# Adaptive-norm block with causal attention and routed experts on one core: setup loads by first use, norms three steps later, slot rows ahead of weights

## The chip, the cores and the metric

The kernel runs on one NeuronCore of a Trainium2 chip: TensorE (PE) for matrix products, VectorE (DVE), ScalarE (ACT) and GpSimd (POOL) for the rest, SyncE (SP) as the queue that issues most transfers, and 16 DMA engines that move data between HBM and the on-chip memory. Each engine runs its own instructions in order, and semaphores tie them together. The metric is the device time of one launch in microseconds (us). Three runs of the kernel before took 746.2, 750.95 and 752.59 us: the median is 750.95.

## The reference, cut to what matters

Eight sequences of 512 tokens of width 128. A conditioning vector per sequence, through SiLU and one matrix, gives six rows: shift, scale and gate for attention and for the feed-forward part. Cut to its core:

```
mod = (silu(c) @ wmod).reshape(8, 6, 1, 128)       # sa, ca, ga, sb, cb, gb; the gates kept >= 0.25 in size
h = layernorm(x) * (1 + ca) + sa
# attention block on h: layer norm; Q, K, V = x U V + b per head, 16 heads of 8, rank 48; causal softmax;
#   out_U out_V + out_b; second layer norm; low-rank MLP with gelu
x = x + ga * attention_block(h)
h = layernorm(x) * (1 + cb) + sb
# feed-forward: RMS norm; a shared MLP with relu; sigmoid router, the best 2 of 8 experts for each token
x = x + gb * (shared(h) + routed(h))
```

All of it is kept in 32-bit floats, but for the attention scores, where Q and K are split into three bf16 parts each.

## The kernel before

**Setup.** SP issues the loads of c, of the matrix w_mod (128 x 768), of the first three sequences of x (512 B per token row) and of the small weights; ACT's queue issues the low-rank factors u_t of Q, K and V (96 rows of 12,288 B, in two halves) and v_t. ACT, DVE and PE form SiLU(c) and its product with w_mod (L1120 the first 256 columns, L1121 the other 512), L1126 spreads the rows of two sequences over the partitions, and L1133 multiplies the low-rank factors of all three of Q, K and V pair by pair (`ps_s2`, 48 products) into `w_qkv`, which DVE copies out (L1554). DVE, with POOL for the reciprocal roots (L738, L740: `var_eps`, `rstd`), norms sequences 0 and 1 before the steps begin. `gates()` (L1520 to L1531) makes the gates from the other columns. `small_weights` (L1155 to L1158) multiplies out_U out_V and the two low-rank factors of the MLP, and DVE copies the results out (L1566 to L1570).

**Attention.** One step n for each group of four heads of one sequence, 32 groups in all, from step -9 on: a table of offsets (`T_AT`, `Q_AT`, ..., `STATS_AT`, `NORM_AT`) says in which step, counted from 4b, each piece of work for sequence b is done. In a step PE makes the first scores of group n+3 (L1205, L1208) that DVE reduces to row maxima (L1620, 12 per step); POOL splits the maxima into bf16 parts (L799 to L807), PE transposes them (L1214), ACT empties them (L987), and SP stores them in HBM and loads them into the Q stack (L575, L585). The second scores of group n (L1232, L1236) then carry their maximum, ACT takes exponentials (L958), and PE makes the context (L1253). Between these, PE transposes, projects and splits the next sequence: Q and K go through ACT, POOL (L787, L791; DVE for sequence 0) and SP (L545 to L551 store them, `load_stack` at L565 and L567 loads them as stacks). The norms of sequences 2 to 7 are four pieces of DVE work in four successive steps (`layer_norm`, after the 4th and the 8th row maximum): statistics of x; scale and shift; statistics of h; normalise. ACT also writes zeros and ones into the Q stacks and the V tiles (L942, L945) before the first step. POOL's step ends with the roots, then adds the two biases to h (L840, L847) where they are due, behind the context's normalisation (L825).

**Experts.** After the MLP and the shared part, tokens are scattered by POOL into regions of HBM by expert (L880), SP pads each region by 132 KB of filling rows (L694, L696, 8 of them), and 39 tiles of 256 slots run: SP loads the tile's rows (`load_slots`, L703, L704) and its expert's weights (`load_weights`, L711 to L713, 514 KB and 64 KB) into four buffers, PE turns the rows (L1390), multiplies (L1428, L1438), ACT and DVE finish, and POOL scatters the results (L926). Before tile 0's second product PE also finishes the shared part of sequences 6 and 7 (L1346): the turn of tile 0 stands ahead of the last 16 of these products in PE's queue.

## Time and profile before

| what | value |
|---|---|
| median of 3 runs | 750.95 us (746.2 to 752.59) |
| the profiled execution's own time | 749.43 us |
| its span, first to last instruction | 747.6 us |
| mean granted TensorE clock | 0.94 of full |
| busy: PE, DVE, ACT, POOL | 624.8, 443.2, 421.0, 304.7 us |
| first exponential of the attention | 75.8 us after the start |
| first product of the expert tiles (L1428) | 570.7 us |

The profile gives, for one execution, the busy time of every engine, the chain of waits that ended last, groups of instructions with their durations and what released the engine before them, and the transfers with the time from issue to landing. A busy PE is not PE at its peak, so shares over the whole span say little; what bounds a stage is read in that stage. Setup lasts until the first exponential, attention until about 395 us, the MLP, shared part and routing until about 560 us, and the expert tiles until about 710 us.

### The profile page before, as it was taken

To read this page: it belongs to the slowest core of one execution; us is meant where nothing else is said; L and a number is where in the kernel's file an instruction comes from. 1 tells how busy PE (TensorE), PEld (TensorE's weight loads), DVE (VectorE), ACT (ScalarE), POOL (GpSimd) and SP (SyncE) were. 2 spreads that over 40 slices of the span, in tenths; PEclk is the share of its full clock that TensorE was granted. 3 is DMA by queue.
4 is the path that set the end of the run, shared out by engine and by line. 5 is a ranking of instruction groups with operands and counts; after the bars stand their busy time and mean duration, and the time that the engine had idled before them with its cause. 6 is when DMAs were issued, how large, how long until landed. Compare 5 with 4: busy or idle time off the path is not lost.

```text
span 747.6 us, 15319 instructions
## 1 busy us (share of the span) xinstructions
PE 624.8 (84%) x5334; PEld 413.5 (55%) x5365; DVE 443.2 (59%) x1306; ACT 421.0 (56%) x749; POOL 304.7 (41%) x490
## 2 busy tenths in 40 slices
PE   4756899998998989999979777887976999999940
PEld 3523444444444544444436464666746899999930
DVE  2689687878788766777606676666741222222227
ACT  5321667676666657666675767775423555555510
POOL 4141424143433415131314276755740454455541
PEclk9958999999999999999999988998997999999975
DMA  8542232333243423331834112111163777777827
GB/s 176 190 162 75 80 123 98 133 133 108 100 158 108 150 91 132 133 106 50 247 118 126 54 46 73 52 47 44 59 164 95 228 229 230 229 226 228 229 104 267
DMA packets 85853, 100.97 MB, mean 135 GB/s; under 512 B 12960, under 2 KB 68040, under 8 KB 85680
## 3 DMA queue, kind: packets, MB, share of 16 engines
q1 hardware_dynamic: 76752, 87.19, 37.9%
q0 software_dynamic: 4544, 9.45, 3.5%
q10 hardware_dynamic: 4480, 3.35, 1.9%
q8 instruction: 43, 0.70, 0.4%
q14 instruction: 34, 0.28, 0.1%
HBM read 60.28 MB, written 37.57 MB: 131 GB/s over the span
## 4 chain that ended last, share of the span: by engine, by line
PE 52%; DVE 12%; DMA 10%; SPq 8%; issue 6%; POOL 5%; ACT 5%; another core or an unknown queue 0%; POOLq 0%; ACTq 0%; DVEq 0%
PE ps_r L1438 8%; PE ps_s L1428 8%; PE ps_pv L1253 7%; DVE row_max L1620 4%; PE ps_r L1208 4%; PE ps_pv L1324 3%; PE ps_r L1205 3%; PE ps_s L1316 3%; DMA arena<-slots_d 3%; PE ps_s L1236 2%; PE ps_r L1346 2%; PE ps_s L1332 2%; DMA k_d<-arena_early 2%; PE ps_pv L1346 2%; PE ps_r L1183 2%
## 5 line engine op out<-in xcount | busy, mean ns | idle before, releaser
L1620 DVE TENSOR_REDUCE row_max<-ps_r 128x1 f32<-128x384 f32 (+3 forms) x384 | 207.0, 595 | 67.6 <-PE ps_r L1208 59.5
L958 ACT ACTIVATE arena<-ps_s 128x1024 f32<-128x1024 f32 (+1 forms) x192 | 159.1, 880 | 64.0 <-PE ps_s L1236 63.1
L1205 PE MATMUL ps_r<-later_q,ident_b 128*128 128x128 bf16 (+1 forms) x384 | 92.5, 247 | 29.8 <-DVE row_max L1620 18.2
L926 POOL DMA_INDIRECT y_d<-arena,target x78 | 74.7, 957 | 94.8 <-DVE arena L1813 82.6
L1208 PE MATMUL ps_r<-arena 128*128 128x128 bf16 (+3 forms) x481 | 112.1, 302 | 0.0
L1205 PEld LDWEIGHTS ps_r<-later_q,ident_b 128*128 128x128 bf16 x384 | 36.1, 98 | 90.2 <-DVE row_max L1620 43.5
L1253 PE MATMUL ps_pv<-arena 128*32 128x512 f32 (+3 forms) x1024 | 83.3, 444 | 0.1
L1809 DVE TENSOR_TENSOR arena<-ps_r,arena_early 128x256 f32<-128x256 f32 x39 | 16.6, 425 | 107.6 <-PE ps_r L1438 107.6
L880 POOL DMA_INDIRECT slots_d<-arena,slots x64 | 65.0, 1015 | 27.5 <-issue 17.7
L1236 PE MATMUL ps_s<-arena 51*128 51x256 bf16 (+3 forms) x512 | 60.2, 300 | 0.0
L1208 PEld LDWEIGHTS ps_r<-arena 128*128 128x128 bf16 x512 | 51.3, 100 | 13.9 <-issue 3.2
L1438 PEld LDWEIGHTS ps_r<-arena 128*128 128x128 f32 x480 | 58.2, 192 | 1.5
L1438 PE MATMUL ps_r<-arena 128*128 128x128 f32 x480 | 58.3, 275 | 0.0
L1110 ACT ACTIVATE arena<-ps_s,arena 128x256 f32<-128x256 f32 x120 | 50.4, 471 | 13.5 <-PE ps_s L1428 12.8
L1428 PE MATMUL ps_s<-arena 128*128 128x256 f32 x240 | 56.8, 379 | 0.0
L799 POOL TENSOR_SCALAR neg_part<-row_max 128x16 bf16<-128x16 f32 x32 | 8.2, 256 | 99.4 <-DVE row_max L1620 99.4
L1428 PEld LDWEIGHTS ps_s<-arena 128*128 128x128 f32 x240 | 43.3, 190 | 4.6
L1253 PEld LDWEIGHTS ps_pv<-arena 128*32 128x32 f32 x1024 | 26.9, 110 | 32.2 <-issue 25.8
L1232 PE MATMUL ps_s<-ident_h,lower_k 64*128 64x64 bf16 (+1 forms) x384 | 40.0, 205 | 5.4 <-ACT arena L958 4.9
L738 POOL TENSOR_TENSOR var_eps<-moments,ln_eps 128x4 f32<-128x4 f32 x24 | 4.9, 202 | 86.3 <-DVE moments L1449 86.3
L1232 PE MATMUL ps_s<-ident_h,upper_k 64*128 64x64 bf16 (+1 forms) x384 | 38.9, 199 | 0.0
L1324 PE MATMUL ps_pv<-w_fc,arena 128*128 128x128 f32 x256 | 33.9, 296 | 5.5 <-ACT arena L1048 5.5
(221 smaller groups left out, 1113.1 us busy)
## 6 DMA issues: line engine op xcount, KB each, us to landing
arena<-in_ew SPq DMA_DIRECT2D x30, 514.0 KB
ctx_d<-ctx_raw SPq DMA_DIRECT2D x32, 256.0 KB, 3.4
arena<-q_d SPq DMA_DIRECT2D x64, 102.0 KB
arena<-k_d SPq DMA_DIRECT2D x64, 96.0 KB
arena<-slots_d SPq DMA_DIRECT2D x39, 132.0 KB, 3.2
arena_early<-in_ew SPq DMA_DIRECT2D x9, 514.0 KB
arena<-y_d SPq DMA_DIRECT2D x8, 512.0 KB, 6.2
q_d<-arena_early SPq DMA_DIRECT2D x8, 384.0 KB, 3.0
```

What stands on the lines that cost most here:

```text
L880: pool.indirect_dma_start(slots_d[:], bass.IndirectOffsetOnAxis(ap=slots[:, c, i:i + 1], axis=0), n3x[:, c, i, :], None).then_inc(scattere ...
L926: pool.indirect_dma_start(y_d[:], bass.IndirectOffsetOnAxis(ap=target[:, k, c:c + 1], axis=0), res[:, k, c, :], None).then_inc(put[k], 16)
L958: act.activation(dst, src, ACT.Exp, scale=SCALE).then_inc(exp_done, 1)
L1205: pe.matmul(diag, ident_b[:], later_q[:].unsqueeze(1).to_broadcast([P, len(js), P]), start=True, stop=False, skip_group_check=True)
L1208: mm = pe.matmul(bnk[:, k * keys:(k + 1) * keys], q_st[b % 2][:, g, j, i * P:(i + 1) * P], k_st[b % 2][:, g, j // 2, 0:keys], start=False, ...
L1232: pe.matmul(banks[half][:, :, at:at + HALF], stationary[whole], near, start=(at == 0), stop=False, skip_group_check=True)
L1236: mm = pe.matmul(banks[j % 2][:, k // 2, :], k_st[b % 2][rows, g, j // 2, kt * P:(kt + 1) * P], q_st[b % 2][rows, g, j, kt * P:S], start=F ...
L1253: mm = pe.matmul(ps_pv[32 * j:32 * j + 32, kt * P:S], v_sb[b % 2][:, kt, GROUPS * j + g, :], probs[:, p % 2, at:at + length], start=(kt == ...
L1324: mm = pe.matmul(ps_pv[:, i * P:(i + 1) * P], hidden[:, k, i * P:(i + 1) * P], w_fc2[:, k, :], start=(k == 0), stop=(k == NF - 1))
L1428: mm = pe.matmul(ps_s2[:, 2 * (k % 2) + f // 2, (f % 2) * SLOTS:(f % 2 + 1) * SLOTS], x_w[k][:, f * P:(f + 1) * P], tok_t[:, k], start=Tru ...
L1438: mm = pe.matmul(ps_s1[:, k % 2, c * P:(c + 1) * P], x_hidden[:, k, f, c * P:(c + 1) * P], x_w[k][:, FF + f * D:FF + (f + 1) * D], start=( ...
L1620: dve.reduce_max(row_max[:, m % 2, js[0] % 2, j:j + len(js), i], src, AXIS.X).then_inc(max_taken, 1)
```

## The change

**Setup loads.** SP's first loads become c, x of sequence 0, the first 256 columns of w_mod, the small columns, x of sequence 1, the other 512 columns of w_mod. u_t is loaded without V's third at first (rows of 8,192 B), V's third follows on ACT's queue behind the exponential of c. The product with w_mod waits only for its 256 columns. The products with the other 512 columns and those of V's pairs move on PE into `small_weights`, behind the first projections of Q and K; ACT in place of DVE empties three of the small weights and writes the V tiles' ones there. `gates()` moves behind DVE's step -3, and the store of its rows from step -3 to -2. Sequence 2 is normed in setup as well, and the four pieces of norm work for sequences 3 to 7 each stand three steps later.

**First stack.** The stores of sequence 0's Q have a semaphore of their own, so that the loads of group 0's Q rows go out before K's stores have landed.

**Experts.** SP issues four fillings, the weights of tile 0, four more fillings, then waits for the fillings and the scatters, then the rows of tiles 0 and 1 and the weights of 1, rows of 2, weights of 2, and so on; before, all four weights went ahead of the wait and of all rows.

```diff
 T_AT, Q_AT, K_AT, K_OUT_AT, LOAD_AT, V_AT = -9, -9, -8, -7, -6, -3
 CTX_AT, REC_AT, OUT_AT = 6, 7, 8
 AFTER_STATS_AT, AFTER_NORM_AT, AFTER_T_AT, AFTER_OUT_AT = 9, 10, 10, 11
-NORM_EARLY = 2
-SMALL_STEP, BIAS_STEP, MOD_STEP = -7, -4, -3
-STATS_AT, SCALE_AT, H_STATS_AT, NORM_AT = -16, -15, -14, -13
+NORM_EARLY = 3
+SMALL_STEP, BIAS_STEP, MOD_STEP = -7, -4, -2
+STATS_AT, SCALE_AT, H_STATS_AT, NORM_AT = -13, -12, -11, -10
...
-                    sp.dma_start(w_mod, a["w_mod"]).then_inc(c_loaded, 16)
-                    for b in range(2):
-                        sp.dma_start(x_sb[:, NT * b:NT * (b + 1), :], x_tok[:, NT * b:NT * (b + 1), :]).then_inc(x_loaded[b], 16)
+                    sp.dma_start(x_sb[:, 0:NT, :], x_tok[:, 0:NT, :]).then_inc(x_loaded[0], 16)
+                    sp.dma_start(w_mod[:, 0:2 * D], a["w_mod"][:, 0:2 * D]).then_inc(w_mod_loaded, 16)
+                    sp.dma_start(cols[:], a["cols"]).then_inc(cols_loaded, 16)
+                    sp.dma_start(x_sb[:, NT:2 * NT, :], x_tok[:, NT:2 * NT, :]).then_inc(x_loaded[1], 16)
+                    sp.dma_start(w_mod[:, 2 * D:6 * D], a["w_mod"][:, 2 * D:6 * D]).then_inc(small_loaded, 16)
...
+                            stored_q = q_stored if b == 0 else qk_stored
+                            sp.dma_start(dst[:, 0:3], part[:, 0:3]).then_inc(stored_q, 16)
+                            sp.dma_start(dst[:, 3:5], part[:, 0:2]).then_inc(stored_q, 16)
+                            sp.dma_start(dst[:, 5:6], part[:, 0:1]).then_inc(stored_q, 16)
...
-                    def load_stack(b, g):
-
-                        wait(sp, qk_stored, 16 * 6 * (b + 1))
+                    def load_stack(b, g, of="qk"):
+
+                        if b == 0:
+                            sp.wait_ge(q_stored, 48)
+                        if "k" in of:
+                            sp.wait_ge(qk_stored, 16 * (6 * b + 3))
...
-                                load_stack(b, g)
+                                load_stack(b, g, "k" if b == 0 and g == 0 else "qk")
...
+                            if batch_at(n, K_OUT_AT) == 0:
+                                load_stack(0, 0, "q")
...
-                    sp.wait_ge(fill_known, 1)
-                    for e in range(E):
-                        at = sp.value_load(fill_at[0:1, e:e + 1], min_val=N_REGION * SLOTS * e, max_val=N_REGION * SLOTS * e + B * S)
-                        chunk = (SPARE_ROWS + SLOTS * e) // P
-                        sp.dma_start(slots_d[bass.ds(at, SLOTS), :].rearrange("(c p) w -> p c w", p=P), fill[:, chunk:chunk + SLOTS // P, :])\
-                            .then_inc(slots_filled, 16)
-
                     def load_slots(t):
 
...
+                    sp.wait_ge(fill_known, 1)
+                    for e in range(E // 2):
+                        store_fill(e)
                     sp.wait_ge(mapped, 2)
-                    for t in range(BUF):
+                    load_weights(0)
+                    for e in range(E // 2, E):
+                        store_fill(e)
+                    sp.wait_ge(scattered, 2 * 16 * B * NT)
+                    sp.wait_ge(slots_filled, 16 * (E + 1))
+                    load_slots(0)
+                    for t in range(1, BUF):
+                        load_slots(t)
                         load_weights(t)
-                    sp.wait_ge(slots_filled, 16 * (E + 1))
-                    sp.wait_ge(scattered, 2 * 16 * B * NT)
-                    for t in range(BUF):
-                        load_slots(t)
...
-                    for b in range(2):
+                    for b in range(NORM_EARLY):
                         x_rstd_of(b)
...
-                        act.dma_start(u_t[HALF * half:HALF * half + RANK], a["u_t"][rows]).then_inc(pairs_loaded, 16)
+                        act.dma_start(u_t[HALF * half:HALF * half + RANK, 0:2], a["u_t"][rows, 0:2]).then_inc(pairs_loaded, 16)
                         act.dma_start(v_t[HALF * half:HALF * half + RANK], a["v_pairs"][half]).then_inc(pairs_loaded, 16)
-                    act.wait_ge(c_loaded, 32)
+                    act.wait_ge(c_loaded, 16)
                     act.activation(c_exp, c_t, ACT.Exp, scale=-1.0).then_inc(c_exped, 1)
+                    for half in range(2):
+                        rows = slice(RANK * half, RANK * half + RANK)
+                        act.dma_start(u_t[HALF * half:HALF * half + RANK, 2], a["u_t"][rows, 2]).then_inc(small_loaded, 16)
                     act.wait_ge(v_zeroed, 1)
                     for stack in q_st:
                         act.activation(stack[:].rearrange("p g j s -> p (g j s)").bitcast(F32), zeros[:, 0:1].to_broadcast([P, GROUPS * JH * S // 2]), ACT.Copy)\
                             .then_inc(q_zeroed, 1)
-                    for v in v_sb:
-                        act.activation(v[:].rearrange("p i h e -> p (i h e)"),
-                                       zeros[:, 0:1].to_broadcast([P, NT * HEADS * 32]), ACT.Copy, bias=1.0).then_inc(v_ones, 1)
+                    def ones_of_v():
+                        for v in v_sb:
+                            act.activation(v[:].rearrange("p i h e -> p (i h e)"),
+                                           zeros[:, 0:1].to_broadcast([P, NT * HEADS * 32]), ACT.Copy, bias=1.0).then_inc(v_ones, 1)
 
...
+                        if n == SMALL_STEP:
+                            ones_of_v()
+                            act.wait_ge(small_done, 1)
+                            act.activation(w_out[:], ps_s2[:, 0, 0:D], ACT.Copy).then_inc(small_copied, 1)
+                            act.activation(w_fc1[:], ps_s2[:, 2, :], ACT.Copy).then_inc(small_copied, 1)
+                            act.activation(w_fc2[:].rearrange("p k d -> p (k d)"), ps_s2[:, 3, :], ACT.Copy).then_inc(small_copied, 1)
...
+                    pe.wait_ge(w_mod_loaded, 16)
                     pe.matmul(ps_m[0:B, 0:2 * D], c_silu, w_mod[:, 0:2 * D], start=True, stop=True).then_inc(mod_done, 1)
-                    pe.matmul(ps_pv[0:B, 0:512], c_silu, w_mod[:, 2 * D:6 * D], start=True, stop=True).then_inc(mod_done, 1)
                     pe.wait_ge(consts2, 1)
                     pe.wait_ge(mod_copied, 1)
                     pe.wait_ge(mod_ready, 1)
                     for b in range(2):
                         pe.matmul(wide_rows(b), ident[0:B, b:b + 1].to_broadcast([B, P]), mod[:, 0:2, :], start=True, stop=True).then_inc(mod_wide, 1)
+
+                    def pairs(*ms):
+                        for m in ms:
+                            for k in range(PAIRS):
+                                for half in range(2):
+                                    rows = slice(HALF * half, HALF * half + RANK)
+                                    at = DH * (PAIRS * m + k)
+                                    mm = pe.matmul(ps_s2[:, half, at:at + DH], u_t[rows, m, k, :], v_t[rows, m, k, :], start=True, stop=True)
+                        mm.then_inc(pairs_done, 1)
+
                     pe.wait_ge(pairs_loaded, 64)
-                    for m in range(3):
-                        for k in range(PAIRS):
-                            for half in range(2):
-                                rows = slice(HALF * half, HALF * half + RANK)
-                                at = DH * (PAIRS * m + k)
-                                mm = pe.matmul(ps_s2[:, half, at:at + DH], u_t[rows, m, k, :], v_t[rows, m, k, :], start=True, stop=True)
-                    mm.then_inc(pairs_done, 1)
+                    pairs(0, 1)
...
                         pe.wait_ge(small_loaded, 16 * SMALL)
+                        pairs(2)
+                        pe.matmul(ps_pv[0:B, 0:512], c_silu, w_mod[:, 2 * D:6 * D], start=True, stop=True).then_inc(mod_done, 1)
                         pe.wait_ge(w_qkv_ready, 6)
...
-                    dve.wait_ge(pairs_done, 1)
-                    for m in range(3):
+
+                    def keep_pairs(m):
                         order = "p (e k t) -> p t k e" if m < 2 else "p (k t e) -> p t k e"
                         kept = w_qkv[:, m, :].rearrange(order, k=PAIRS, t=2)
                         for half in range(2):
                             at = PAIRS * DH * m
                             dve.tensor_copy(kept[:, half], ps_s2[:, half, at:at + PAIRS * DH].rearrange("p (k e) -> p k e", e=DH))\
                                 .then_inc(w_qkv_ready, 1)
+
+                    dve.wait_ge(pairs_done, 1)
+                    keep_pairs(0)
+                    keep_pairs(1)
                     norm_all(1)
+                    stats_all_x(2)
 
                     for m in range(2):
                         dve.wait_ge(act_emptied, BY_ACT["QK"[m], 0] + 1)
...
                         dve.wait_ge(qk_mid, m + 1)
                         dve.tensor_tensor(qk_part[:, m, 2], qk_rest[:, m], qk_part[:, m, 1], ALU.subtract).then_inc(qk_low, 1)
                     normalise_all(1)
-                    gates()
-                    dve.wait_ge(small_done, 1)
-                    dve.tensor_copy(w_out[:], ps_s2[:, 0, 0:D]).then_inc(small_copied, 1)
+                    dve.wait_ge(pairs_done, 2)
+                    keep_pairs(2)
+                    norm_all(2)
                     dve.wait_ge(cols_loaded, 16)
                     dve.tensor_scalar(vb_wide, zeros[:], col("v_b"), None, ALU.add).then_inc(small_copied, 1)
-                    dve.tensor_copy(w_fc1[:], ps_s2[:, 2, :]).then_inc(small_copied, 1)
-                    dve.tensor_copy(w_fc2[:].rearrange("p k d -> p (k d)"), ps_s2[:, 3, :]).then_inc(small_copied, 1)
+                    dve.wait_ge(mod_done, 2)
+                    dve.tensor_copy(mod[:, 2:6, :], ps_pv[0:B, 0:512].rearrange("b (k d) -> b k d", d=D)).then_inc(mod_copied, 1)
+                    normalise_all(2)
 
...
+                        if n == MOD_STEP - 1:
+                            gates()
```

Three places where the order of instructions moves. First, TensorE at the program's start (`ps_m` is `ps_r`, `ps_pv` takes the 512 columns; `in_*` and `arena` hold the loaded weights). Before:

```order
L1120 MATMUL ps_r<-arena 8x256 [waits silu_ready]
L1121 MATMUL ps_pv<-arena 8x512
L1126 MATMUL ps_s<-arena,ident 128x256 [waits mod_ready,mod_copied,consts2]
L1126 MATMUL ps_s<-arena,ident 128x256
L1133 MATMUL ps_s<-arena 128x8 [waits pairs_loaded]
L1133 MATMUL ps_s<-arena 128x8 x47
L1169 MATMUL ps_r<-ident,arena_early 128x128 [waits xn_ready,consts2]
```

And now:

```order
L1147 MATMUL ps_r<-arena 8x256 [waits w_mod_loaded,silu_ready]
L1152 MATMUL ps_s<-arena,ident 128x256 [waits mod_ready,mod_copied,consts2]
L1152 MATMUL ps_s<-arena,ident 128x256
L1160 MATMUL ps_s<-arena 128x8 [waits pairs_loaded]
L1160 MATMUL ps_s<-arena 128x8 x31
L1201 MATMUL ps_r<-ident,arena_early 128x128 [waits xn_ready,consts2]
```

The 512-column product and 16 of the 48 pair products have left the stretch ahead of the first transposes; they stand behind the projections of Q and K.

Second, GpSimd ahead of the first split of row maxima: the Q and K remainders of sequence 1 (`arena_early` tiles) and the roots of the norms. Before:

```order
L738 TENSOR_TENSOR var_eps<-moments,ln_eps 128x4 [waits h_moments]
L740 TENSOR_TENSOR rstd<-var_eps,half_neg 128x4 [waits h_eps]
L787 TENSOR_TENSOR arena_early<-arena_early 128x512 [waits qk_low,act_emptied]
L791 TENSOR_TENSOR arena_early<-arena_early 128x512 [waits qk_mid]
L787 TENSOR_TENSOR arena_early<-arena_early 128x512 [waits qk_low,act_emptied]
L738 TENSOR_TENSOR var_eps<-moments,ln_eps 128x4 [waits x_moments]
L740 TENSOR_TENSOR rstd<-var_eps,half_neg 128x4 [waits x_eps]
L791 TENSOR_TENSOR arena_early<-arena_early 128x512 [waits qk_mid]
L799 TENSOR_SCALAR neg_part<-row_max 128x16 [waits max_taken]
```

And now:

```order
L752 TENSOR_TENSOR var_eps<-moments,ln_eps 128x4 [waits h_moments]
L754 TENSOR_TENSOR rstd<-var_eps,half_neg 128x4 [waits h_eps]
L796 MEMSET rms_eps 128x4
L797 MEMSET per_d 128x4
L801 TENSOR_TENSOR arena_early<-arena_early 128x512 [waits qk_low,act_emptied]
L805 TENSOR_TENSOR arena_early<-arena_early 128x512 [waits qk_mid]
L801 TENSOR_TENSOR arena_early<-arena_early 128x512 [waits qk_low,act_emptied]
L805 TENSOR_TENSOR arena_early<-arena_early 128x512 [waits qk_mid]
L813 TENSOR_SCALAR neg_part<-row_max 128x16 [waits max_taken]
```

The root of sequence 3 no longer stands between the remainders of sequence 1; that of sequence 2 still stands ahead of them.

Third, SyncE's queue ahead of the expert tiles (`in_ew` the expert's weights, `slots_d` the sorted rows). Before:

```order
L711 TENSOR_LOAD tile_expert [waits mapped]
...
L712 DMA arena<-in_ew 128x1028
...
L713 DMA arena_early<-in_eb 128x128
...
L712 DMA arena_early<-in_ew 128x1028
...
L703 TENSOR_LOAD tile_row [waits scattered,slots_filled]
...
L704 DMA arena<-slots_d 128x264
```

And now:

```order
L713 TENSOR_LOAD tile_expert [waits mapped]
...
L714 DMA arena<-in_ew 128x1028
...
L721 DMA slots_d<-arena 128x2x132
...
L705 TENSOR_LOAD tile_row [waits slots_filled,scattered]
...
L706 DMA arena<-slots_d 128x264
L705 TENSOR_LOAD tile_row
...
L706 DMA arena<-slots_d 128x264
L713 TENSOR_LOAD tile_expert
```

Three of the four weight loads ahead of tile 0's rows are now behind them, and four of the fillings are behind the first weights.

## Rows read from the trace of the kernel before

**Rows 1.** Transfers issued in the first 60 us: issues, KB each, median us to landing
```profile
arena<-in_u_t ACTq DMA_DIRECT2D x2, 576.0 KB, 8.7
x_sb<-in_x SPq DMA_DIRECT2D x3, 256.0 KB, 12.1
arena<-in_w_mod SPq DMA_DIRECT2D x1, 384.0 KB, 7.5
arena<-in_c_t SPq DMA_DIRECT2D x1, 4.0 KB, 4.4
```

**Rows 2.** Chain of waits, 0 to 80 us: start, us, what
```profile
1.23 7.54 DMA arena<-in_w_mod
...
9.70 1.02 PE ps_r L1120 x2
10.72 1.71 PE ps_pv L1121 x2
12.43 2.00 PE ps_s L1126 x4
14.43 10.34 PE ps_s L1133 x96
...
46.86 1.12 POOL arena_early L787
...
51.27 1.01 POOL rstd L740
...
65.63 4.51 DMA max_d<-max_rows
```

**Rows 3.** Instructions in order of time: start, us, engine, line, [idle before, releaser]
```profile
15.92 3.69 ACT L945 ACTIVATE arena<-zeros 128x2048 f32<-128x2048 f32 x2
...
31.89 1.05 PE L1158 MATMUL ps_s<-arena 64*128 64x128 f32 x8
...
34.69 1.11 DVE L1483 TENSOR_SCALAR arena_early<-h_sb,moments,rstd 128x128 f32<-128x128 f32 x4
...
37.84 2.07 PE L1183 MATMUL ps_r<-arena_early,w_qkv 128*128 128x512 f32 x2 [0.87 <-ACT arena_early L965]
...
38.53 0.67 DVE L1569 COPY w_fc<-ps_s 128x512 f32<-128x512 f32 x1
```

**Rows 4.** The same view in the attention steps: DVE in step 0
```profile
83.40 1.02 DVE L1620 TENSOR_REDUCE row_max<-ps_r 128x1 f32<-128x384 f32 x2 [3.33 <-PE ps_r L1208]
```

**Rows 5.** Chain of waits, 78 to 260 us: the shift of a norm in step 1
```profile
94.81 1.05 DVE h_sb L1472 x4
```

**Rows 6.** GpSimd in order of time, 165 to 245 us: steps 11 and 15
```profile
198.02 1.26 POOL L840 TENSOR_TENSOR h_sb<-h_sb,fc_bias 128x512 f32<-128x512 f32 x1
...
200.49 0.25 POOL L799 TENSOR_SCALAR neg_part<-row_max 128x16 bf16<-128x16 f32 x1
...
242.47 0.25 POOL L799 TENSOR_SCALAR neg_part<-row_max 128x16 bf16<-128x16 f32 x1 [1.34 <-DVE row_max L1620]
```

**Rows 7.** Instructions in order of time ahead of the expert tiles, 540 to 606 us
```profile
544.22 8.58 SPq L696 DMA_DIRECT2D slots_d<-arena  x8
...
553.57 0.38 SPq L712 DMA_DIRECT2D arena<-in_ew  x1
...
560.55 4.74 SPq L704 DMA_DIRECT2D arena<-slots_d  x5
565.50 0.69 PE L1390 MATMUL ps_r<-ident,arena 128*128 128x128 f32 x2 [8.58 <-DMA arena<-slots_d]
```

**Rows 8.** The fillings' line L696, 540 to 566 us
```profile
DMA to landing us min/median/max: 2.1/2.3/2.8
```

**Rows 9.** The page's transfers: all 39 loads of slot rows, KB each, median us to landing
```profile
arena<-slots_d SPq DMA_DIRECT2D x39, 132.0 KB, 3.2
```

**Rows 10.** Windows: busy us of PE, PEld, DVE, ACT, POOL; granted clock, DMA share, GB/s
```profile
560.10:570.20 10.10, 4.10 (x18) 3.81 (x18) 0.56 (x1) 0.47 (x1) 0.00 (x0) 0.50 0.56 180
...
650.00:700.00 50.00, 49.93 (x346) 46.76 (x345) 12.81 (x52) 28.92 (x68) 25.69 (x27) 1.00 0.78 228
```

35 lines of the change are left out of this document (19 added, 16 removed).

## The prediction

> **What bounds the kernel now.** I read the chain of waits first, then the instructions in order of time around its long pieces, then the transfers and the windows. Three stretches matter.
>
> Setup, 0 to 80 us. The chain begins with the landing of w_mod, which is issued at 1.23 us and takes 7.54 us [rows 2]; SiLU follows, then four stretches of PE without a gap: the 256-column product (1.02), the 512-column product (1.71), the spread of rows (2.00) and the pair products (10.34 for 96 passes, 0.108 us each), which end at 24.77 us [rows 2]. From there it runs through ACT and PE to POOL, whose remainder of sequence 1 starts at 46.86 us [rows 2], and through SP's stores and loads to the first maximum's store at 65.63 us [rows 2]. That store blocks ACT, and with it PE's transposes of sequence 2; the first exponential comes at 75.8 us. So setup is a latency chain: an edit counts only where it shortens this chain.
>
> Attention steps, about 10.3 us each. PE and DVE are both in the chain; DVE's norm work shows there in pieces [rows 5], but in steps that project K it waits for PE, once 3.33 us [rows 4].
>
> Experts. In 650 to 700 us PE is busy 49.93 of 50 us at a DMA share of 0.78 [rows 10]: the tiles are bound by PE, and what can be won is their start. PE idles 8.58 us for the first tile's rows and turns them at 565.50 [rows 7].
>
> **The change part by part.**
>
> *Loads and pair products.* The 256-column product starts at 9.70 us now. Afterwards the exponential needs only c, which lands 4.4 us after its issue [rows 1], so SiLU is done by about 6.1, and the 256 columns of w_mod (128 KB) decide. Ahead of them stand 256 KB of x in rows of 512 B, so as many bytes as now (384 KB) must pass on SP's queue before they have landed. By bytes they land at 8.8 us like w_mod now (1.23 + 7.54), and the product starts 0.9 us early. But x took 12.1 us to land and finished only with u_t [rows 1]: small rows pass slowly beside u_t's long ones. If the x rows wait for u_t again, which is two thirds as long, the columns land at about 11. I take a start at 9.7 as now, between 8.8 and 11.
>
> Then the 512-column product is gone from the path. Now the spread of rows starts 12.43 − 9.70 = 2.73 us after the first product; without it, it must wait for that product (1.02) and DVE's two copies (about 0.5 us), so 1.55: **1.2 us** gained. Of 96 pair passes 32 move: 32 x 0.108 = **3.45 us**. The spread then ends at 13.2 and the pairs at 20.2. DVE's norm of sequence 0 was hidden behind the pairs and nearly is still: x has landed, statistics start at 11.2, and by the same durations as now the normalised rows are ready at 19.7. Cover left: 0.5 us. Sum 4.6 us; I take **4.5**, bounds 3.2 and 5.8 (by the landing).
>
> *From the projections to the first maximum's store*, in today's times. The moved pair products (3.45 us) and the 512 columns (1.7) run on PE from about 30.3 to 35.5, beside the split of Q and K; DVE normalises sequence 1 till 35.8 [rows 3], copies V's pairs (0.3), and PE's small weights (2.6 us long, ending now at 32.94 [rows 3]) end at 38.7. ACT's ones (3.69 us [rows 3]) lie in 34.05 to 37.7 before that, covered by 1.0 us. ACT empties the small weights in 0.27 + 2 x 0.67 = 1.6 us (DVE's duration [rows 3], for ACT's I have none) till 40.3, then sequence 1's transposes (0.79), PE projects Q (2.07 at the lower clock [rows 3]) till 43.2, ACT's two copies take 1.3: POOL can start at 44.5. Now it starts at 46.86 [rows 2], since it waits for the root of sequence 2, whose norm DVE begins only at 39.72; after the change that root is done at 40.8. Gain 2.4 us. Then the root of sequence 3 (1.24 us with its addition [rows 2]) no longer stands between the remainders. Gain 1.2. SP is free in time, since group 0's Q rows go out during K's stores. Sum **3.6 us**, bounds 1.5 and 5 (PE at either clock, and SP's 16 stack loads). The first steps' DVE work is 5.7 us lighter (one sequence's norm), and `gates()` adds 1.8 between two of them; the maximum's own path ends by 60 us, before SP is ready for it at 62. So the first exponential comes 4.5 + 3.6 = **8.1 us** early.
>
> *Norms three steps later.* Nothing is added; each piece meets other work. The shift (1.05 us in the chain [rows 5]) leaves the steps that project V for the ones that project K, where DVE waits for PE anyway [rows 4]; statistics take its place. In GpSimd's queue the root of x now stands behind the context's normalisation, which waits for a transfer, and ahead of L840 and L847: in step 11 they end at 200.49 and delays the next maximum already [rows 6], so 1.25 us are lost there, while in step 15 it has 1.34 us to spare [rows 6]. Sequence 7's norm falls on steps 15 to 18, which had less. I set gains of 0.7 us in four steps against 1.25 + about 1.5 and take **0**, bounds +4 lost and 3 gained.
>
> *Experts.* Fillings come every 1.17 us from 544.22 (8 in 8.58 [rows 7]), weights every 1.7 (four between 553.57 and 560.55 [rows 7]). Four fillings, one weight (issued at 548.8), four fillings: the last issue is at 553.9, landed 2.8 us later at the most [rows 8], 556.7; the last of POOL's scatters ends its issue at 552.9, so it isn't later. The tile number's load takes 0.7, so tile 0's rows go out at 557.4, not 560.55. They took 4.9 us then, queued behind three to four weights of 514 KB; the median of all 39 such loads is 3.2 [rows 9]. With one weight ahead, long landed, I take 3.2: the turn comes at 560.7 and not 565.5: **4.8 us**, bounds 3.1 (if the load still takes 4.9) and 5.5. The weights of tiles 1 to 3 go out at about 559, 562 and 564.5; PE wants them at 567.7, 571.4 and 575 (3.73 us per tile). The clock doesn't help: it was at the lower level, 0.50 of full, from 560.10 to 570.20 [rows 10], after PE had idled from 556.9, and PE will idle 3.7 us still.
>
> Sum: 8.1 + 0 + 4.8 = 12.9 us. The profiled execution took 749.43 us, so 736.5; the median of the runs is 1.5 us above it, which would give 738. I predict **737 us**.
>
> A rule of the Trainium skill speaks about the first term (DMA: Bandwidth & Descriptors, Queues, rings and completion order): a DMA engine takes turns between queues packet by packet, a packet being some 9 to 17 descriptors, so that x's small rows would not be held up row for row by u_t's long ones. The landing of x with u_t [rows 1] speaks against it; by the rule the sum would be 2.7 us better, as the fourth case below.
>
> **The rivals.**
>
> 1. *The front is eaten downstream* (12%). The stack loads or K's stores land later because everything now goes out closer together, and the first maximum's store stays near 63 us. For it: the chain passes four transfers here. Then about 2 us of the 8.1 remain: 749.4 − 2 − 4.8 = 742.5.
> 2. *The tiles start early and starve* (10%). Weights of tiles 1 to 3 share the engines with rows and put PE to wait: 710 KB per tile at 228 GB/s [rows 10] are 3.1 us, so 3.7 us of slack must be used up. All of the 4.8 us would go: 741.5.
> 3. *Slower* (5%). GpSimd's queue in every fourth step: the root of x can start only after DVE's 8th maximum, and L840, L847 and the next split wait behind it. Full price 1.25 + 1.26 + 1.27 = 3.8 us (L847 takes as long as L840 [rows 6]) in steps 3, 7, 11 and 15, 15.2 us, and the shift in the K steps shows in full, 5 x 1.05. 749.4 − 12.9 + 20.4 = 757. It decides from the point where the split ends more than about 4 us after DVE's last maximum, where PE transposes; against it stands the slack of step 15 [rows 6].
> 4. *Columns early* (10%). The 256 columns land at 7, beside u_t. The spread starts at 8.6, pair products wait for u_t till 10.6, and end at 17.5 instead of 20.2: 734.
> 5. *It doesn't do what it says* (3%): all the waits are replaced by others, 749.
>
> The forecast has 60%, with its own range of 731 to 743: the bounds of the four terms seldom meet at one end.
>
> **How the numbers follow.** About 1% (7.5 us) is what a measurement of this kernel can tell from no change, so faster means under 743.4. The forecast and case 4 give nearly all of their 70%, cases 1 and 2 about 13 of 22 points: 82% faster. The rest of these and case 5 make 13% same. Slower 5%. The range reaches from 731 to 745: it takes in case 4 and cases 1 and 2 for the most part, and leaves out case 3, case 5 and the far ends.
>
> **What would show it.** The 256-column product near 9.7 us (case 4: near 7), and the first transposes of sequence 0 near 20.2. POOL's first remainder of sequence 1 near 40, the first maximum's store near 57.5, the first exponential near 67.7. Distances of the maxima's splits in attention as before within 0.5 us, with steps 11 and 15 the ones to look at. The turn of tile 0 4.8 us closer to the first filling's store than now (21.3 us), and no wait of PE for weights in tiles 1 to 3. I would be wrong if PE's pair products wait for u_t or x, if ACT's ones hold up the transposes of sequence 1, or if the gain at the first exponential isn't there any more when the attention ends.

## The result: 0.994 of the time before, where 0.98 was forecast

| | before | after |
|---|---|---|
| median of the runs | 751.26 us (20 runs) | 747.61 us (20 runs) |
| ratio, 95% interval | | 0.9942 (0.9920 to 0.9963) |
| profiled execution, span | 749.43, 747.6 us | 749.93, 748.1 us |

In a second comparison, where all kernels ran on one chip (`all_before`, `all_after` below), the ratio was 0.9931 (0.9903 to 0.9959). So the change gains 4 to 5 us. Forecast were 737 us and a range up to 745; the time lies outside it.

### Profile after: setup

The chain of waits of the changed kernel, 0 to 80 us (start, us, what); these answer to [rows 2]:

```profile
1.70 8.07 DMA arena<-in_w_mod
...
9.91 1.03 PE ps_r L1147 x2
...
11.59 2.04 PE ps_s L1152 x4
13.62 6.93 PE ps_s L1160 x64
20.55 1.06 PE ps_r L1201 x4
...
34.70 1.72 PE ps_s L1190 x8
...
41.87 1.16 POOL arena_early L801
...
59.65 4.25 DMA max_d<-max_rows
```

The 256 columns land at 9.77 us, their product starts at 9.91 (9.70 before), and the first transposes come at 20.55, where the pairs before ended at 24.77: 4.2 us earlier. The remainder of sequence 1 starts 5.0 us earlier (41.87 against 46.86), the first maximum's store 6.0 (59.65 against 65.63). The first exponential comes at 69.6 us, 6.2 earlier than 75.8.

One piece of this chain is longer than before. The two passes of one product of the small weights (L1156 before, L1188 after), in order of time:

```profile
30.88 1.17 PE L1156 MATMUL ps_s<-arena 64*128 64x512 f32 x2
32.63 2.07 PE L1188 MATMUL ps_s<-arena 64*128 64x512 f32 x2
```

All the small weights together (12 passes) took 2.6 us before and take 4.5 now (31.90 to 36.41). They take 4.5 in every trace of a kernel with the new setup, e1_norms_back and the later ones included, and 2.6 to 3.1 in the four traces with the old one. The cause is TensorE's lower clock: the clock rows of the changed kernel's first trace don't begin until 51 us, but in seven of the others they cover this stretch, and read 0.50 of full, as in e1_norms_back (PE, PEld, DVE, ACT, POOL busy, then the granted clock, DMA share, GB/s):

```profile
32.20:36.70 4.50, 4.48 (x13) 2.99 (x13) 3.88 (x18) 1.55 (x1) 1.22 (x4) 0.50 0.57 190
```

### Profile after: attention

What follows uses one number per step: the distance from one split of maxima to the next, taken between the starts of GpSimd's first row of each split (L799 before, L813 after; 32 of them). The length of step n runs from the split that ends step n-1 to the one that ends step n; the first split ends step -3, the last one step 28. The first split is 6.8 us earlier than before; the last is 6.8 us later (377.77 against 370.99). Steps 1 to 28, called "attention" in what follows, take 294.5 us (83.31 to 377.77), before 282.8 (88.23 to 370.99). **Here the gain of setup goes, and as much again.**

GpSimd in order of time at the end of step 11 (start, us, engine, line, operation; in brackets the idle time before it and its releaser); it answers to [rows 6]:

```profile
196.45 1.27 POOL L839 TENSOR_TENSOR ctx_n<-ctx_t,rec_rows 128x512 f32<-128x512 f32 x1 [5.51 <-DMA rec_rows<-rec_d]
197.67 0.20 POOL L752 TENSOR_TENSOR var_eps<-moments,ln_eps 128x4 f32<-128x4 f32 x1
197.95 1.04 POOL L754 TENSOR_TENSOR rstd<-var_eps,half_neg 128x4 f32<-128x4 f32 x1
198.96 1.27 POOL L854 TENSOR_TENSOR h_sb<-h_sb,fc_bias 128x512 f32<-128x512 f32 x1
200.20 1.26 POOL L861 TENSOR_TENSOR h_sb<-h_sb,out_bias 128x512 f32<-128x512 f32 x1
201.43 0.26 POOL L813 TENSOR_SCALAR neg_part<-row_max 128x16 bf16<-128x16 f32 x1
```

No gap between them: the root's two instructions stand in the chain between a transfer (`rec_rows`) and the next split. In step 15 the same rows run from 242.94 to 247.97, and the split that had 1.34 us to spare before [rows 6] has none.

DVE and GpSimd in order of time in step 4, which projects K:

```profile
115.14 2.04 DVE L1499 SCALAR_TENSOR_TENSOR arena_early<-x_sb,moments,arena_early 128x128 f32<-128x128 f32 x4
115.76 1.27 POOL L805 TENSOR_TENSOR arena_early<-arena_early 128x512 bf16<-128x512 f32 x1 [0.74 <-ACT arena_early L996]
...
118.72 1.02 DVE L1656 TENSOR_REDUCE row_max<-ps_r 128x1 f32<-128x384 f32 x2 [0.62 <-PE ps_r L1240]
119.66 2.03 DVE L1504 SCALAR_TENSOR_TENSOR h_sb<-arena_early,rstd 128x128 f32<-128x128 f32 x4
119.85 1.17 POOL L801 TENSOR_TENSOR arena_early<-arena_early 128x512 f32<-128x512 f32 x1 [2.82 <-ACT arena_early L992]
121.62 2.47 DVE L1656 TENSOR_REDUCE row_max<-ps_r 128x1 f32<-128x512 f32 x4
...
122.35 0.23 PE L1237 MATMUL ps_r<-later_q,ident_b 128*128 128x128 bf16 x1 [1.53 <-DVE row_max L1656]
```

And the same group of four shifts in the kernel before, in step 5, which projects V:

```profile
134.75 1.13 DVE L1472 SCALAR_TENSOR_TENSOR h_sb<-arena_early,rstd 128x128 f32<-128x128 f32 x4
```

Step 4 of the kernel before, which has no shift, shows where DVE waits for TensorE: 0.92 us ahead of the 7th maximum, and only 0.28 behind the 8th:

```profile
124.10 1.02 DVE L1620 TENSOR_REDUCE row_max<-ps_r 128x1 f32<-128x384 f32 x2 [0.92 <-PE ps_r L1208]
125.03 0.37 DVE L1449 BATCH_NORM_AGGREGATE moments<-stats 128x2 f32<-128x6 f32 x4
125.68 2.49 DVE L1620 TENSOR_REDUCE row_max<-ps_r 128x1 f32<-128x512 f32 x4 [0.28 <-PE ps_r L1208]
```

Two things are to be seen. In the changed kernel DVE's wait for TensorE still stands ahead of the 7th and 8th maxima (0.62 us), and the shifts stand behind the 8th: they fill no such wait, they make TensorE wait (1.53 us). And four shifts take 2.03 us, not 1.13, while GpSimd's L801 runs beside them. By the line's own view for 119 to 122 us, one of the four took 1247 ns and the others about 340:

```profile
L1504 DVE SCALAR_TENSOR_TENSOR h_sb<-arena_early,rstd x4: 338/341/1247, 119.7 to 121.4; 128x128 f32<-128x128 f32 x4
```

The scale of this step (L1499) meets GpSimd's L805 in the same way and takes 2.04 us. That costs nothing here: e9_shift_sixth below keeps it (2.03 us), and its step 4 is as short as before.

### Profile after: experts

Instructions in order of time, 548 to 575 us; these answer to [rows 7]:

```profile
550.55 3.85 SPq L721 DMA_DIRECT2D slots_d<-arena  x4
...
556.91 4.13 SPq L721 DMA_DIRECT2D slots_d<-arena  x4
...
564.00 1.50 SPq L706 DMA_DIRECT2D arena<-slots_d  x2
...
566.25 0.53 PE L1422 MATMUL ps_r<-ident,arena 128*128 128x128 f32 x2 [2.97 <-DMA arena<-slots_d]
```

From the first filling's store to the turn of tile 0 it is 15.7 us now, 21.3 before: 5.6 us gained, 4.8 forecast. TensorE waits 2.97 us for the rows and not 8.58. The rows of tile 0 go out 13.5 us after the first filling, where 13.2 were forecast, and are turned 2.3 us later, where 3.2 were set. From tile 0's first product to the end of the span it is 176.9 us in both kernels.

### The profile page after: what moved, and what is told of

The parts are those of the page before. It is cut to its first block, busy times and chain, and to the rows that moved or that the text cites. A ratio compares the mean times of both kernels' runs of the same rounds, so it can differ in the third digit from the quotient of the medians.

```text
span 748.1 us, 15358 instructions
## 1 busy us (share of the span) xinstructions
PE 631.9 (84%) x5365; PEld 416.7 (56%) x5365; DVE 445.9 (60%) x1303; ACT 421.2 (56%) x752; POOL 306.6 (41%) x490
## 4 chain that ended last, share of the span: by engine, by line
PE 42%; DMA 16%; SPq 12%; DVE 10%; POOL 8%; issue 6%; ACT 5%; POOLq 0%; ACTq 0%; DVEq 0%
PE ps_r L1470 7%; PE ps_s L1460 7%; PE ps_pv L1285 4%; DMA max_d<-max_rows 4%; PE ps_pv L1356 3%; DMA arena<-slots_d 3%; DVE row_max L1656 3%; DMA k_d<-arena_early 2%; SPq L571 2%; PE ps_s L1348 2%; PE ps_r L1378 2%; SPq L574 2%; PE ps_r L1215 2%; PE ps_s L1364 2%; PE ps_r L1240 2%
## 5 line engine op out<-in xcount | busy, mean ns | idle before, releaser
L1240 PE MATMUL ps_r<-arena 128*128 128x384 bf16 (+3 forms) x512 | 121.3, 310 | 0.0
L1285 PE MATMUL ps_pv<-arena 128*32 128x512 f32 (+3 forms) x1024 | 85.0, 450 | 0.1
L813 POOL TENSOR_SCALAR neg_part<-row_max 128x16 bf16<-128x16 f32 x32 | 8.3, 260 | 112.7 <-DVE row_max L1656 112.5
L1356 PE MATMUL ps_pv<-w_fc,arena 128*128 128x128 f32 x256 | 35.8, 307 | 3.9 <-ACT arena L1074 3.9
L1356 PEld LDWEIGHTS ps_pv<-w_fc,arena 128*128 128x128 f32 x256 | 34.7, 221 | 6.4 <-ACT arena L1074 6.4
```

Of the source, the lines that this page charges most:

```text
L1240: mm = pe.matmul(bnk[:, k * keys:(k + 1) * keys], q_st[b % 2][:, g, j, i * P:(i + 1) * P], k_st[b % 2][:, g, j // 2, 0:keys], start=False, ...
L1285: mm = pe.matmul(ps_pv[32 * j:32 * j + 32, kt * P:S], v_sb[b % 2][:, kt, GROUPS * j + g, :], probs[:, p % 2, at:at + length], start=(kt == ...
L1356: mm = pe.matmul(ps_pv[:, i * P:(i + 1) * P], hidden[:, k, i * P:(i + 1) * P], w_fc2[:, k, :], start=(k == 0), stop=(k == NF - 1))
```

## The experiments

The length of single steps, and of attention (steps 1 to 28), in us. K marks the steps that project K.

| kernel | 4 (K) | 5 | 7 | 8 (K) | 11 | 12 (K) | 15 | 16 (K) | attention |
|---|---|---|---|---|---|---|---|---|---|
| before | 10.51 | 10.11 | 9.85 | 10.81 | 11.55 | 10.51 | 11.35 | 10.55 | 282.8 |
| after | 11.82 | 10.94 | 11.04 | 11.82 | 12.03 | 11.84 | 13.51 | 11.83 | 294.5 |
| e1_norms_back | 10.52 | 10.10 | 9.74 | 10.82 | 11.74 | 10.52 | 11.45 | 10.53 | 284.1 |
| e2_shift_alone | 11.82 | 9.39 | 11.03 | 11.81 | 12.42 | 11.83 | 13.34 | 11.82 | 292.4 |
| e5_root_first | 11.83 | 9.39 | 9.75 | 12.11 | 11.27 | 11.82 | 12.08 | 11.83 | 287.5 |
| e6_stats_only | 10.53 | 10.11 | 10.67 | 10.53 | 12.64 | 10.53 | 11.59 | 10.53 | 285.4 |
| e7_scale_in_k | 11.81 | 9.39 | 10.48 | 11.90 | 12.08 | 12.37 | 11.25 | 10.51 | 290.2 |
| e8_bias_moved | 10.52 | 10.17 | 10.13 | 10.82 | 10.16 | 10.82 | 11.03 | 10.82 | 283.3 |
| e9_shift_sixth | 10.53 | 9.39 | 10.56 | 10.89 | 11.80 | 10.53 | 12.80 | 10.54 | 284.6 |
| e12_no_collision | 10.92 | 9.39 | 10.86 | 10.93 | 12.05 | 10.95 | 12.78 | 10.93 | 285.8 |
| e10_both | 10.51 | 9.39 | 9.75 | 10.89 | 11.25 | 10.65 | 12.03 | 10.64 | 282.4 |
| all_before | 10.51 | 10.10 | 10.17 | 10.81 | 11.55 | 10.54 | 12.21 | 10.51 | 283.5 |
| all_after | 11.82 | 9.39 | 10.87 | 11.81 | 12.11 | 11.81 | 13.47 | 12.93 | 290.3 |

The two traces of the kernel before show how far a step can be trusted: the K steps and step 5 agree within 0.04 us, steps 7 and 15 only within 0.3 and 0.9.

Ratios are to the kernel before on the same chip (medians there: 753.6 for e1 to e4, 751.2 for e5 to e8, 766.0 for e9 to e12, 751.7 for the last four).

### The parts apart

`e1_norms_back`, the changed kernel with one line undone:

```diff
-STATS_AT, SCALE_AT, H_STATS_AT, NORM_AT = -13, -12, -11, -10
+STATS_AT, SCALE_AT, H_STATS_AT, NORM_AT = -16, -15, -14, -13
```

> The changed kernel with one line undone: the four pieces of norm work at offsets -16, -15, -14, -13 again, sequence 2 still normed in setup. Theory A (the new places lengthen the attention steps: the root of x stands ahead of L854 and L861 in GpSimd's queue in every fourth step, and scale and shift stand in the steps that project K): the 13 us that attention lost between the first split of maxima and step 17 come back, about 735 us (733 to 738), and the splits keep their lead of about 6 us over the kernel before to the end of the attention. Theory B (attention is paced by something that a 6 us earlier start cannot move, so the lead would be eaten wherever the norms stand): about 747, as the changed kernel.

Measured: ratio 0.9828 (0.9798 to 0.9858), 13.0 us less than before; the lead at the last split is 2.8 us. Theory A holds (attention 284.1), B falls. The 735 us were not reached (741.7, where before is 753.6), as the size was taken from one trace and the lead was not kept whole: with sequence 3's norm back in the first steps, the first split comes 2.2 us later than in the changed kernel, so the later norms help ahead of step 0.

`e2_shift_alone` is the kernel before with the opposite edit:

> The kernel before with that one line alone changed: offsets -13, -12, -11, -10, sequence 2's norm included. Theory A: 751.3 + 13 = 764 (760 to 767), the added time in the steps up to 17. Theory B: about 751, since no lead is there to be eaten.

Measured: ratio 1.0107 (1.0074 to 1.0141), 8 us slower; attention 9.6 us longer. A's direction is right, its 13 us too much. The kernel has no lead to lose, so this excludes theory B a second time.

`e3_experts_alone`, the kernel before with SyncE's new order ahead of the tiles:

```diff
+for e in range(E // 2): store_fill(e)
 sp.wait_ge(mapped, 2)
-for t in range(BUF): load_weights(t)
-sp.wait_ge(slots_filled, 16 * (E + 1)); sp.wait_ge(scattered, 2 * 16 * B * NT)
-for t in range(BUF): load_slots(t)
+load_weights(0)
+for e in range(E // 2, E): store_fill(e)
+sp.wait_ge(scattered, 2 * 16 * B * NT); sp.wait_ge(slots_filled, 16 * (E + 1))
+load_slots(0)
+for t in range(1, BUF): load_slots(t); load_weights(t)
```

> The kernel before with the new order of SyncE ahead of the expert tiles alone. From the traces of both kernels, first filling's store to first product of tile 0: 26.5 us before, 20.7 after, so 5.8 us less: about 745.5 (744 to 748). If the tiles starve for weights instead, 750 or above.

Measured: ratio 0.9881 (0.9847 to 0.9915), 9 us less; the trace shows 5.6 (filling to first product 20.9 us, 26.5 before). The interval's near end is 6.4; what the rest is, no trace shows. The tiles don't starve.

`e4_setup_alone` is e1_norms_back with the old order of SyncE ahead of the tiles:

> The new setup and first stack with sequence 2 normed in setup, norm offsets and experts as before. The first maximum's store was 6.0 us earlier in the changed kernel and the first exponential 6.2: theory A says 751.3 - 6.2 = 745 (743 to 747). Theory B: 750 or above, since the lead is eaten in the attention.

Measured: ratio 0.9903 (0.9878 to 0.9927), 7.3 us less, as A says. e3 and e4 add up to 16.3 where both together (e1) gave 13.0: within their intervals, and not settled closer.

### What in the later norms costs

`e5_root_first`, the changed kernel with GpSimd's root of x ahead of the context's normalisation:

```diff
+later = batch_at(n, STATS_AT)
+if later is not None and later >= NORM_EARLY:
+    x_rstd_of(later)
 if batch_at(n, REC_AT) is not None:
     ...
     pool.tensor_tensor(ctx_n[:], ctx_t[:], rec_rows[:], ALU.mult)
 ...
-for offset, of in ((STATS_AT, x_rstd_of), (H_STATS_AT, h_rstd_of)):
+for offset, of in ((H_STATS_AT, h_rstd_of),):
```

> The changed kernel with the root of x (L752, L754) issued on GpSimd ahead of the context's normalisation (L839), for which GpSimd waits 5 to 7 us there anyway. Theory C (the root stands in the chain, 1.24 us before L854, L861 and the next split): steps 7, 11 and 15 (11.04, 12.03, 13.51 us from split to split) shorten by 1.0 to 1.25 each, the kernel by 3 us. Theory D (DVE's statistics of x, moved into the same steps, are what lengthens them): they keep their lengths within 0.3 and the time stays.

GpSimd at the end of step 15 of this kernel:

```profile
237.61 0.20 POOL L752 TENSOR_TENSOR var_eps<-moments,ln_eps 128x4 f32<-128x4 f32 x1 [5.51 <-DVE moments L1484]
237.90 1.04 POOL L754 TENSOR_TENSOR rstd<-var_eps,half_neg 128x4 f32<-128x4 f32 x1
238.95 1.26 POOL L842 TENSOR_TENSOR ctx_n<-ctx_t,rec_rows 128x512 f32<-128x512 f32 x1
240.17 1.27 POOL L857 TENSOR_TENSOR h_sb<-h_sb,fc_bias 128x512 f32<-128x512 f32 x1
241.40 1.28 POOL L864 TENSOR_TENSOR h_sb<-h_sb,out_bias 128x512 f32<-128x512 f32 x1
242.64 0.26 POOL L813 TENSOR_SCALAR neg_part<-row_max 128x16 bf16<-128x16 f32 x1
```

The root now lies in what was waiting. Steps 7, 11 and 15 are 1.3, 0.8 and 1.4 us shorter than in the changed kernel: theory C, though by more than the 1.0 to 1.25 expected in two steps and by less in one. The whole time hardly moved (0.9929, 0.9900 to 0.9958): in this profile step -1 took 12.4 us in place of 8.8, with TensorE's granted clock at 0.50 of full (1.2 of 2.4 GHz) from 65 to 70 us, so this run alone doesn't show the gain at the end.

`e6_stats_only` and `e7_scale_in_k` move one piece at a time, starting from e1_norms_back:

```diff
-STATS_AT, SCALE_AT, H_STATS_AT, NORM_AT = -16, -15, -14, -13
+STATS_AT, SCALE_AT, H_STATS_AT, NORM_AT = -17, -15, -14, -13   # e6_stats_only
+STATS_AT, SCALE_AT, H_STATS_AT, NORM_AT = -17, -16, -14, -13   # e7_scale_in_k
```

> As e1_norms_back, but the statistics and the root of x one step earlier (-17 in place of -16), so that this piece alone stands in the steps 3, 7, 11 and 15, as in the changed kernel. If this piece makes their added length: steps 7, 11 and 15 as in the changed kernel (11.0, 12.0, 13.5 us; 9.7, 11.7, 11.5 in e1_norms_back), 3 to 4 us more in all. If normalise's leaving them pays for it in the changed kernel and not here, 1 us more than that. Steps 0, 4, 8, 12 and 16 as in e1_norms_back or shorter by up to 0.3.

> As e6_stats_only, but scale and shift one step earlier too (-16), so that they stand in the steps that project K (4, 8, 12, 16), as in the changed kernel. If DVE's shift between two maxima makes the 1.3 us there: steps 4, 8, 12 and 16 1.3 us longer than in e6_stats_only (10.5 to 11.8 where measured from step 4), the steps behind them 0.75 shorter: 2 to 3 us more in all. My prediction had DVE waiting for PE there, so nothing added and 1.05 us less in the steps behind: 3 us less.

Measured: e6 0.9881 (0.9851 to 0.9911), e7 0.9884 (0.9857 to 0.9912). e6: steps 7 and 11 are 0.9 us longer than in e1_norms_back. Step 15 is only 0.1 longer, but it says nothing of the root: in this kernel no statistics and no root of x stand there (GpSimd runs only L839, L854 and L861), against what was expected of the edit. Attention is 1.3 us longer, where 3 to 4 were expected. e7: steps 4, 8 and 12 are 1.3, 1.4 and 1.8 us longer than in e6; step 16, which holds no shift in this kernel, is unchanged; step 5 is 0.7 shorter; attention 4.7 us more, a part of which is the lower clock, which fell in steps 8 and 12 (3.4 us at 0.50 each). So scale and shift in a K step cost 1.3 us: the opposite of the prediction. The two ratios don't tell them apart; the steps do.

`e9_shift_sixth` and `e12_no_collision` ask why. e9 issues the shifts after the 6th maximum. e12 leaves them behind the 8th, but GpSimd's L801 waits for them:

```diff
-if u in (3, 7):
+if u in (3, 5, 7):        # e9: scale at u == 3, shift at u == 5, all other pieces as before
     layer_norm(n, u)
```

```diff
 if b is not None:
+    shifted = batch_at(n, SCALE_AT)          # e12
+    if shifted is not None and shifted >= NORM_EARLY:
+        pool.wait_ge(h_ready, NT * (shifted + 1))
     qk_remainder(b, 1)
```

> The changed kernel with the four shifts (L1504) after the 6th row maximum of their step in place of the 8th. In step 4 of the changed kernel DVE waits 0.62 us for TensorE between the 6th and 8th maxima, and the shifts behind the 8th take 2.03 us (1.13 in the kernel before), with GpSimd's L801 (1.17 us) running beside them from 119.85. Theory F (the shift costs because it stands behind the wait and collides with L801): after the 6th maximum it takes 1.13 us and fills the wait, so steps 0, 4, 8, 12 and 16 go from 11.8 to about 10.5 us, and the kernel is 5 to 6.5 us faster than the changed one. If all DVE work in such a step costs its own time wherever it stands: 11.8 stays, or at most 0.3 less.

> The changed kernel, shifts after the 8th maximum as there, but GpSimd's second remainder (L801) of these steps waits for them. It tells the collision from the place. If the two engines exclude each other, the shifts take 1.13 us in place of 2.03, and steps 4, 8, 12 and 16 go from 11.8 to 10.9; about 4 us less than the changed kernel in all. If it is the place alone: 11.8 or above, since L801 starts 1 us later and nothing is won.

DVE in step 4 of e9_shift_sixth, with GpSimd's L801:

```profile
116.74 1.01 DVE L1658 TENSOR_REDUCE row_max<-ps_r 128x1 f32<-128x384 f32 x2
...
117.67 1.13 DVE L1504 SCALAR_TENSOR_TENSOR h_sb<-arena_early,rstd 128x128 f32<-128x128 f32 x4
118.72 1.01 DVE L1658 TENSOR_REDUCE row_max<-ps_r 128x1 f32<-128x384 f32 x2
119.50 1.16 POOL L801 TENSOR_TENSOR arena_early<-arena_early 128x512 f32<-128x512 f32 x1 [2.82 <-ACT arena_early L992]
```

The shifts of step 4 in e12_no_collision (the line's own view, 120 to 123 us):

```profile
L1507 DVE SCALAR_TENSOR_TENSOR h_sb<-arena_early,rstd x4: 343/346/347, 120.7 to 121.5; 128x128 f32<-128x128 f32 x4
```

e12: the shifts take 1.13 us in all five places and the K steps 10.92 to 10.95 where 10.9 was expected. **So 0.9 us of the 1.3 is the collision.** e9: steps 4, 12 and 16 take 10.53 us (step 8 takes 10.89, before 10.81), the wait ahead of the 7th maximum is filled, and the rest of the 1.3 is gone too. Ratios 0.9812 (0.9773 to 0.9851) for e9 and 0.9838 (0.9795 to 0.9880) for e12; the changed kernel wasn't run on that chip, so the steps carry this, not the ratios. Against `all_after` attention is 5.7 and 4.5 us shorter, where 5 to 6.5 and 4 were expected.

Of this the Trainium skill has the rule (SBUF — State Buffer, Who interferes with whom): VectorE and GpSimd share one pair of ports under an exclusive lock, and a VectorE instruction with two SBUF inputs contends with a GpSimd one that reads SBUF. The rows agree: the shifts read `scaled` and `mod_sb`, both in SBUF, and one was held up for 0.9 us while L801 ran 1.17. Row maxima, which read PSUM, were not held up: the 128x512 ones of the attention took 680 ns in the middle with a GpSimd `tensor_tensor` beside them (49) and 679 without (63).

### Other placements

`e8_bias_moved`:

```diff
-b = batch_at(n, AFTER_OUT_AT)      # L854, 11
+b = batch_at(n, AFTER_NORM_AT)     # 10
...
-b = batch_at(n, 3)                 # L861
+b = batch_at(n, 1)
```

> As e1_norms_back, but GpSimd's two additions of a bias to h (L854, L861; 1.26 us each) leave the steps 3, 7, 11 and 15: L861 two steps earlier, L854 one step earlier, where GpSimd waits for DVE. If GpSimd's queue behind the context's normalisation sets the length of steps 11 and 15 with the norms in their old places too: these go from 11.7 and 11.5 us to about 10, so 3 us less than e1_norms_back in all. If the transfer that the normalisation waits for sets it, or another engine: the same within 1 us.

Measured: ratio 0.9824 (0.9796 to 0.9852), as e1_norms_back. Step 11 fell to 10.16 and step 15 to 11.03, but steps 0 and 24 grew by 0.8 and 2.2 us: attention is only 0.8 us less, where 3 were expected. A queue relieved in one step was paid for in others. It also shows the hold-up once more: in step 5, L861 (1.37 us) now runs beside the scale, which took 2.15 us in place of 1.13:

```profile
L1499 DVE SCALAR_TENSOR_TENSOR arena_early<-x_sb,moments,arena_early x4: 339/342/1367, 128.1 to 129.9; 128x128 f32<-128x128 f32 x4
```

`e11_back_sixth` is e1_norms_back with the shifts after the 6th maximum:

> As e1_norms_back with the shifts after the 6th maximum, in the steps that project V (5, 9, 13). There GpSimd runs nothing beside them and DVE waits 0.4 to 0.5 us: at most 0.4 us per step for each of five, so e1_norms_back within 2 us.

Measured: ratio 0.9805 (0.9763 to 0.9847); steps 5, 9 and 13 are 0.3 to 0.5 us shorter, attention 281.0. `e10_both` has both repairs, with the norms in their new places:

> e5_root_first and e9_shift_sixth together: root of x ahead of the context's normalisation, shifts after the 6th maximum. If these two are the whole price of the new places, attention from step 1 on takes as long as before (282.8 us, against 294.5 in the changed kernel), and the whole is 737 to 740 where before is 751, as e1_norms_back. If normalise in its new place (steps 6, 10, 14) has a price of its own: 1 to 2 us more.

Attention takes 282.4 us, as the kernel before; ratio 0.9778 (0.9738 to 0.9819). That chip is slower: the kernel before took 766.0 us there. e10_both is the one kernel with a trace there and one on another chip (`all_e10`): its spans differ by 11.9 us, and the stretch from the last split to the first filling's store by 12.0 (184.3 and 172.3), attention by 0.4.

### All on one chip

> The kernel before, as a run of its own on the chip of the next three. Steps 1 to 27 of the attention take 282.8 us as in the first trace, within 1 us (they are set by the program); if the whole time is not 747 to 751, the difference lies outside these steps.

> The changed kernel on the same chip. Ratio to before 0.994 as first measured; attention from step 1 to 28 between 291 and 295 us, by how many steps fall to the lower clock. If the later norms cost what attention shows, it stands 10 to 12 us above all_e1; if what the first ratios say, 8 to 9.

> e1_norms_back on the same chip: ratio 0.98, attention from step 1 to 28 within 1.5 us of before.

> e10_both on the same chip, norms in their new places. If GpSimd's queue and the shift are the whole price: 282.4 us of attention and within 2 us of all_e1, on either side. If normalise in its new place costs too: 2 to 4 us above it.

| kernel | median | ratio, 95% | attention |
|---|---|---|---|
| all_before | 751.77 | 1.0007 (0.9981 to 1.0034) | 283.5 |
| all_after | 747.23 | 0.9931 (0.9903 to 0.9959) | 290.3 |
| all_e1 | 739.88 | 0.9850 (0.9815 to 0.9885) | 282.2 |
| all_e10 | 736.26 | 0.9803 (0.9769 to 0.9837) | 282.8 |

The later norms cost 7.4 us by the medians (747.2 to 739.9), 8.1 by attention; 8 to 9 or 10 to 12 were expected. Root first and shift after the 6th maximum take 11.0 us off the changed kernel. all_e10 has the lowest median of the four; its 3.6 us below all_e1 are not settled, since the intervals overlap. It stands at the 737 us that was forecast, but by other terms (see below). Attention differs by 4.2 us between the two traces of the changed kernel. In the first, the clock fell to its lower level at the end of step 4 and the start of step 5, in the second not. The windows 120 to 125 and 125 to 130 us (PE, PEld, DVE, ACT, POOL busy, then the granted clock, DMA share, GB/s) of the first:

```profile
120.00:125.00 5.00, 3.47 (x28) 1.00 (x25) 4.09 (x8) 3.20 (x5) 1.68 (x4) 0.77 0.34 120
125.00:130.00 5.00, 5.00 (x58) 2.44 (x55) 2.86 (x9) 2.40 (x5) 1.66 (x4) 0.88 0.00 0
```

and of `all_after`:

```profile
120.00:125.00 5.00, 3.46 (x35) 1.42 (x34) 4.27 (x10) 2.99 (x5) 1.50 (x6) 1.00 0.20 70
125.00:130.00 5.00, 5.00 (x73) 3.28 (x72) 3.84 (x10) 3.11 (x6) 1.18 (x2) 1.00 0.23 79
```

TensorE was busy 3.5 of 5 us in both; in one it was then granted less, and step 5 took 10.94 us and not 9.39. The same came again from step 12 of the first trace (step 13 takes 11.15 us and not 9.58) and in step 16 of the second. The lengthened K steps seem to bring that risk with them: of the five traces whose K steps take 11.8 us four have a stretch at 0.50 within steps 1 to 28, each begun in a K step (`after`, e2, e7, `all_after`; not e5), and of the other thirteen none has. That is a count of single traces and not an experiment on its own. Behind the attention, the stretch to the first filling's store takes 169.6 to 175.1 us in the four traces of this chip, at a clock of 0.95 to 0.91, though its code is the same: two single profiles don't compare to better than about 5 us.

## Why the prediction was wrong, point by point

- *Loads and pair products, 4.5 us*: 4.2 measured, by the mechanism forecast: product at 9.91, 64 passes in 6.93 us (0.108 each), pairs off the path. The columns landed at 9.77 us, inside the bounds of 8.8 and 11. Case 4 (columns at 7) falls. Its picture was half right: x of sequence 0, issued at 1.24 us, landed 5.5 us later at 6.7, ahead of u_t's second half (issued at 1.71, landed after 7.8), so its small rows did not wait for all of u_t. That x "finished only with u_t" can't be read in [rows 1] either, which has medians. The landing of x agrees with what the Trainium skill says (DMA: Bandwidth & Descriptors, Queues, rings and completion order), that a DMA engine takes turns between its queues. The columns, issued behind x, came 3.1 us after it all the same, 0.2 behind u_t; why is not shown.
- *Projections to the first maximum's store, 3.6 us*: 1.8 measured (6.0 in all at the store, 6.2 at the first exponential). Two terms were mis-sized. TensorE's small weights were taken at 2.6 us, their duration at full clock, and took 4.5 at the lower one (31.90 to 36.41); the work moved ahead of them had ended 0.27 us before DVE released them and lengthened nothing. So the first remainder of sequence 1 gained 0.8 us on top of the 4.2, where 2.4 were set. And the root of sequence 3, gone from between the remainders, gave 0.4 us and not 1.2, as GpSimd now waits there for ACT (from 41.87 to the end of the last remainder at 48.0 it is 6.1 us, before 6.5). K's stores landed 0.5 us faster, which no term had. The splits' lead then fell from 6.8 to 4.9 us by step 1; 1.3 of that is step 0, a K step with a shift. Case 1 (the front eaten downstream) had the right sign for 2 us of this, not its place: it spoke of stores and stack loads.
- *Norms three steps later, 0*: **the step that failed.** It cost 7.4 us (all_after to all_e1), 8 in e2. Two sentences of it failed. That the shift "leaves the steps that project V for the ones that project K, where DVE waits for PE anyway" had both halves true and the conclusion false. The V steps did get 0.7 to 0.8 us shorter (step 5: 9.39 against 10.11), as set. But the wait of [rows 4] stands ahead of the 7th maximum (and its 3.33 us are those of step 0; in step 4 it is 0.92), and the shift behind the 8th, where DVE waited 0.28, so it was added to the path, with 0.4 us; and it ran beside L801, which nearly doubled it and added 0.9. That price was never asked for: a duration was carried to a place where GpSimd runs beside it. That step 15 "has 1.34 us to spare" took the slack from a schedule in which nothing else in that step had moved: with the root in it the step takes 13.5 us, and with the root ahead of the context's normalisation 12.1 (e5), which is no longer than in one of the two traces of the kernel before (11.35 and 12.21).
- *Case 3 (slower), 5%*: it named both places, GpSimd's queue in steps 3, 7, 11 and 15 and the shift in K steps, and priced them at 20.4 us over the forecast. The places were right, the price came to 7 or 8 us: of the steps with a root ahead, step 3 lost nothing. A case that decides by degrees was treated as all or nothing, and the part of it between got no share of the chance.
- *Experts, 4.8 us*: 5.6 from filling to turn, 5.8 to the first product, by the mechanism forecast; the rows came 0.9 us sooner after their issue than set. Case 2 (starving tiles) falls: 176.9 us from the first product to the end in both kernels.
- *The sum*: without the failed term the forecast was 12.9 us; e1_norms_back gave 13.0 (10.7 to 15.2) and all_e1 11.3 (8.6 to 13.9). That they meet is in part luck: setup was 2.1 us short and the experts 0.8 over, and the lead at the last split was 2.8 and 5.4 us where 8.1 were set.
- *Cases 1 and 2* end, by their own terms, at 742.6 and 741.3 us and not at 742.5 and 741.5; nothing hangs on it.
- *The range*: its upper end, 745, took in a loss of 4 us for that term. The measured 747.6 needed 10.6 us of loss on the forecast; the failed term (7.4 to 8) and setup (2.1) make 9.5 to 10.1 of it.

Open stay why the columns landed no sooner, why step 15 takes 11.3 us once and 12.2 another time in the same kernel, and the 3 us by which e3_experts_alone exceeds its trace.

## What to carry to other kernels

A wait on an engine is a gap at one place in its queue: work moved into the step fills it only if it is issued ahead of the instruction that waits. Before a VectorE operation with two SBUF inputs is moved, look at what GpSimd runs at the new time, since one of them then stands still for the other's rest. And a step's slack is to be read in the new schedule: in the new steps root and shift cost 7 to 8 us in all, and nothing (282.4 us of attention against 282.8) once the root was issued ahead of the context's normalisation and the shift ahead of two row maxima. Last, a duration read at one level of the clock (2.6 us) is not that of the same work once it is moved (4.5).

## What was unexpected in the hardware

- One `scalar_tensor_tensor` of 128 x 128 with both inputs in SBUF takes 0.34 us, and 1.25 to 1.37 when a GpSimd `tensor_tensor` of 1.17 to 1.37 us starts just before it; the three others of its group are untouched. What is added is what is left of GpSimd's instruction, less 0.2 us: with 1.10 us left the shift of step 4 took 0.90 more, with 0.52 left the first scale of step 12 took 0.33 more. GpSimd's instruction kept its 1.17 us in both.
- After the same 3.5 us of TensorE work in 5, the granted clock stayed at full once, and fell to 0.50 for 3.4 us once (0.77 in the mean of the 5 us), which made the next step 1.55 us longer.
- From one chip to another the same kernel (e10_both) kept its attention (282.4 and 282.8 us) and differed by 12 us in the stretch behind it.
